# Layer 2's probabilities turned by a transposing DMA, and layer 1's value products and transposes put into one block

## The reference

```python
# layer 1, 12 heads of 64
h = einsum('bnd,ade->bane', x, W)
attn = leaky(tanh(h) @ w_src + swap(tanh(h) @ w_dst), 0.2)
attn = softmax(where(adj, attn, -999.0))
feat = elu(heads_joined(attn @ h + b))
gate = sigmoid(x @ H_w.T + H_b)
x = layernorm(x + gate * feat + (1 - gate) * x)
# layer 2, 6 heads of 128
q, k, v = heads(x @ Wq + bq), heads(x @ Wk + bk), heads(x @ Wv + bv)
probs = softmax(q @ k.T / sqrt(128) + where(adj, 0, -9e15))
x = layernorm(x + heads_joined(probs @ v) @ Wf + bf)
```

## Time and profile before

| | us |
|---|---|
| median of 3 runs | 2765.53 (2763.75 to 2770.96) |
| the profiled execution | 2766.33 |
| its span, first to last instruction | 2764.6 |
| PE busy | 2726.9 (99%) |
| DVE busy | 1668.8 (60%) |
| ACT busy | 1160.3 (42%) |
| POOL busy | 1066.3 (39%) |

### The profile page before, as it was taken

How to read it: one execution, slowest core, us unless ns; L and a number is a source line. 1 busy time by engine, 2 the same in 40 slices (tenths; PEclk the granted TensorE clock), 3 DMA queues, 4 the chain that set the end, 5 groups by cost and what they waited for, 6 DMA issues and landing times.

```text
span 2764.6 us, 51821 instructions
## 1 busy us (share of the span) xinstructions
PE 2726.9 (99%) x20988; PEld 2517.8 (91%) x20988; DVE 1668.8 (60%) x3334; ACT 1160.3 (42%) x3045; POOL 1066.3 (39%) x630
## 2 busy tenths in 40 slices
PE   8999999999999989999999999999999999999998
PEld 6877778888788889999999999999999999999998
DVE  6888998888888754444454444454445445444443
ACT  5666776666666633322332233322332233223322
POOL 2453344433444134433444343434443343434340
PEclk9999999999999999999999999999999999999999
DMA  5656665555555512222213222222222222222220
GB/s 180 173 131 145 164 160 145 139 139 139 141 137 143 175 59 69 69 71 81 70 58 81 76 75 58 79 72 71 69 68 71 81 70 58 81 81 70 58 70 23
DMA packets 306894, 269.49 MB, mean 97 GB/s; under 512 B 227808, under 2 KB 244192, under 8 KB 306656
## 3 DMA queue, kind: packets, MB, share of 16 engines
q1 hardware_dynamic: 306656, 266.19, 35.5%
HBM read 142.65 MB, written 75.89 MB: 79 GB/s over the span
## 4 chain that ended last, share of the span: by engine, by line
PE 85%; DVE 5%; DMA 4%; issue 2%; POOL 2%; ACT 2%; SPq 1%; DVEq 0%; ACTq 0%; POOLq 0%
PE ps_hg L1036 21%; PE ps_a L1199 14%; PE ps_k L70 14%; PE ps_q L70 14%; PE ps_a L70 14%; PE ps_c L1165 2%; PE ps_s L1140 2%; PE ps_pv L1068 1%; DMA dst_all<-dst_scratch 1%; ACT logits L564 1%; PE ps_t L1055 1%; PE ps_pt L1165 1%; DMA dst_scratch<-dst 1%; PE ps_pt L1147 1%; DVE logits L770 1%
## 5 line engine op out<-in xcount | busy, mean ns | idle before, releaser
L1036 PE MATMUL ps_hg<-w_hi,xT 128*128 128x512 f32 x2268 | 745.6, 401 | 8.3 <-DVE h_one L803 8.2
L1036 PEld LDWEIGHTS ps_hg<-w_hi,xT 128*128 128x128 f32 x2268 | 426.1, 188 | 112.6 <-issue 11.3
L1036 PE MATMUL ps_hg<-w_lo,xT 128*128 128x512 f32 x1134 | 448.4, 395 | 0.0
L70 PE MATMUL ps_k<-x1T_hi,wk_hi 128*128 128x256 f32 x1152 | 329.1, 286 | 0.0
L70 PE MATMUL ps_q<-x1T_hi,wq_hi 128*128 128x256 f32 x1152 | 323.5, 281 | 1.4 <-DVE x1T_lo L910 1.4
L70 PE MATMUL ps_q<-x1T_lo,wq_hi 128*128 128x256 f32 x1152 | 322.6, 280 | 0.0
L70 PE MATMUL ps_k<-x1T_lo,wk_hi 128*128 128x256 f32 x1152 | 321.9, 279 | 0.0
L70 PE MATMUL ps_q<-x1T_hi,wq_lo 128*128 128x256 f32 x1152 | 321.9, 279 | 0.0
L70 PE MATMUL ps_k<-x1T_hi,wk_lo 128*128 128x256 f32 x1152 | 321.1, 279 | 0.0
L496 POOL TENSOR_TENSOR th_src<-th,wsrc_all 128x768 f32<-128x768 f32 x64 | 118.3, 1848 | 483.7 <-DVE dst_all L783 463.4
L648 ACT ACTIVATE qT<-ps_q,bq_col 128x256 f32<-128x256 f32 x192 | 80.5, 470 | 479.3 <-PE ps_q L70 479.3
(11 more groups left out here) (144 smaller groups left out, 5814.2 us busy)
## 6 DMA issues: line engine op xcount, KB each, us to landing
x_tok<-x SPq DMA_DIRECT2D x64, 384.0 KB, 4.1
dst_all<-dst_scratch SPq DMA_DIRECT2D x128, 192.0 KB, 3.4
gate_scratch<-gate SPq DMA_DIRECT2D x64, 384.0 KB, 2.6
feat_scratch<-feat SPq DMA_DIRECT2D x128, 192.0 KB, 2.8
feat_in<-feat_scratch SPq DMA_DIRECT2D x62, 384.0 KB, 3.1
gate_in<-gate_scratch SPq DMA_DIRECT2D x62, 384.0 KB, 3.7
x_even<-x SPq DMA_DIRECT2D x16, 768.0 KB, 4.2
x_odd<-x SPq DMA_DIRECT2D x16, 768.0 KB, 4.4
```

The costliest lines, as they stand in the source:

```text
L70: ins = pe.matmul(out, left[a][c], right[b][c], start=(n == 0), stop=(n == len(terms) - 1))
L1036: ins = pe.matmul(ps_hg[:, cols], left[a][c], right[b][c], start=(c == 0 and n == 0), stop=(c == KC - 1 and n == 2))
```

## The change

It has two parts. In layer 2, from group 2 on, the probabilities of each pair are no longer transposed on TensorE: POOL splits `scores_sb` into two 16-bit planes (`split_p1`), SP turns them with a transposing DMA (`turn_p1`), and ACT and DVE join the planes into `probs1T` (`join_block`). POOL's list places the splits around the preparation of the next group's input, and DVE's mix of the second tile moves behind `logits_of(G, 2)` and `probs_out(G, 1)`. In layer 1, `values(T-2)` and `transpose_probs(T-1)` follow each other in the middle of `project(2)`; `copy_probs` moves behind the exponentials of the same tile on ACT, and `bias_h(T)` in front of `attention(T-2)` on DVE.

```diff
+        planes_p1 = at(S + 53184, "planes_p1", [P, 2, PN * NODES], U16)
+        planes_p1T = at(S + 54208, "planes_p1T", [P, 2, 2, P], U16)
...
+        def join_block(copy, buf, t, g, signal):
+            s = graph(g)
+            out_ = probs1T[s, buf, :, s].bitcast(U16).rearrange("p (h t) (n l) -> p l h t n", t=GT, l=2)[:, :, :, t, :]
+            copy(out_, planes_p1T[t * NODES:(t + 1) * NODES, :, :, s]).then_inc(signal, 1)
+        def pair_of(G, j):
+            return PAIRS * (G - BY_DMA) + j + 1
...
# SP
+            def turn_p1(G, j):
+                sp.wait_ge(split_p1_done, pair_of(G, j))
+                for joined_ in (ptc_act, ptc_dve):
+                    sp.wait_ge(joined_, 2 * (PAIRS * G + j))
+                sp.dma_start_transpose(planes_p1T.rearrange("p l h n -> p (l h) n"),
+                                       planes_p1.rearrange("p l (h m) -> p (l h) m", h=2)).then_inc(turned_p1, 16)
...
                     sp.dma_start(x1_tok[s][:, :, :], x_g[G + 2]).then_inc(x1_in[s], 16)
+                if BY_DMA <= G + 1 < NG:
+                    turn_p1(G + 1, 0)
+                if G + 2 < NG:
                     sp.wait_ge(mixed, GT * (G + 2) + 1)
                     feat_and_gate(G + 2, 1)
+                if BY_DMA <= G + 1 < NG:
+                    for j in range(1, PAIRS):
+                        turn_p1(G + 1, j)
...
# POOL
+            def split_p1(G, j):
+                pool.wait_ge(probs_done, PAIRS * G + j + 1)
+                if pair_of(G, j) > 1:
+                    pool.wait_ge(turned_p1, 16 * (pair_of(G, j) - 1))
+                pool.tensor_copy(planes_p1[:, :, :], scores_sb.rearrange("p k m -> p (k m)").bitcast(U16)
+                                 .rearrange("p (d l) -> p l d", l=2)).then_inc(split_p1_done, 1)
...
-                if 1 <= G < NG - 1:
-                    for t in range(GT):
+                for t in range(GT):
+                    if 1 <= G < NG - 1:
                         feat_less_x(G + 1, t, feat_in[:, :])
+                    if G >= BY_DMA:
+                        split_p1(G, t)
+                    if 1 <= G < NG - 1:
                         times_gate(G + 1, t, feat_in[:, :], gate_in[:, :])
+                if G >= BY_DMA:
+                    split_p1(G, GT)
...
# ACT, layer 1
-                if T >= 2:
-                    copy_probs(T - 2)
+                if T == 2:
+                    copy_probs(0)
...
                 exp_scores(T - 1)
                 if T >= 2:
+                    copy_probs(T - 1)
                     elu_exp(T - 2)
...
# ACT, layer 2
                 value_out(G, 0)
-                probs_out(G, 1)
+                if G < BY_DMA:
+                    probs_out(G, 1)
                 exps(G, 2)
+                if G >= BY_DMA:
+                    probs_out(G, 1)
...
# DVE, layer 1
                 dst_scores(T)
                 if T >= 2:
+                    bias_h(T)
                     attention(T - 2)
-                    bias_h(T)
...
# DVE, layer 2 (and logits_of(G, j) now waits for split_p1_done of pair j-1)
-                elif G + 1 < NG:
+                elif G < BY_DMA:
                     mix(G + 1, 1, feat_in[:, :])
                     input_moments(G + 1)
-                probs_out(G, 1)
+                if G < BY_DMA:
+                    probs_out(G, 1)
                 logits_of(G, 2)
+                if G >= BY_DMA:
+                    probs_out(G, 1)
+                    if G + 1 < NG:
+                        mix(G + 1, 1, feat_in[:, :])
+                        input_moments(G + 1)
...
# TensorE, layer 1
                 project(1, T).then_inc(h_done, 1)
+                project(2, T, range(KC // 2))
                 if T >= 2:
                     values(T - 2)
-                project(2, T).then_inc(g_done, 1)
-                if T >= 2:
                     transpose_probs(T - 1)
+                project(2, T, range(KC // 2, KC)).then_inc(g_done, 1)
...
# TensorE, layer 2: scores(G, j) waits for logit_done of pair j-1, and
-                transpose_probs1(G, 0)
+                if G < BY_DMA:
+                    transpose_probs1(G, 0)
```

More of the change, by code:

```diff
@@ L244, in two_graph_layers @@
         turned1 = [sem(f"turned1_{t}") for t in range(GT)]
+        split_p1_done, turned_p1 = (sem(n) for n in ("split_p1_done", "turned_p1"))
         v_done, v_copied, o_done, o_added = (sem(n) for n in ("v_done", "v_copied", "o_done", "o_added"))
@@ L677, in probs_out @@
             def probs_out(G, j):
-                act.wait_ge(pt1_done, PAIRS * G + j + 1)
-                for g in range(2):
-                    copy_block(act.copy, (G + j) % 2, 0, g, ptc_act)
+                if G < BY_DMA:
+                    act.wait_ge(pt1_done, PAIRS * G + j + 1)
+                    for g in range(2):
+                        copy_block(act.copy, (G + j) % 2, 0, g, ptc_act)
+                else:
+                    act.wait_ge(turned_p1, 16 * pair_of(G, j))
+                    for g in range(2):
+                        join_block(act.copy, (G + j) % 2, 0, g, ptc_act)
             def context_hi(G, j):
@@ L687, in _ @@
             round_x1(0)
-            copy_probs(NT - 2)
             leaky_scores(NT - 1)
@@ L916, in logits_of @@
                     dve.wait_ge(bias_mask, G + 1)
+                elif G < BY_DMA:
+                    dve.wait_ge(pt1_done, PAIRS * G + j)
                 else:
-                    dve.wait_ge(pt1_done, PAIRS * G + j)
+                    dve.wait_ge(split_p1_done, pair_of(G, j - 1))
                 dve.scalar_tensor_tensor(
@@ L934, in probs_out @@
             def probs_out(G, j):
-                dve.wait_ge(pt1_done, PAIRS * G + j + 1)
-                for g in range(2):
-                    copy_block(dve.tensor_copy, (G + j) % 2, 1, g, ptc_dve)
+                if G < BY_DMA:
+                    dve.wait_ge(pt1_done, PAIRS * G + j + 1)
+                    for g in range(2):
+                        copy_block(dve.tensor_copy, (G + j) % 2, 1, g, ptc_dve)
+                else:
+                    dve.wait_ge(turned_p1, 16 * pair_of(G, j))
+                    for g in range(2):
+                        join_block(dve.tensor_copy, (G + j) % 2, 1, g, ptc_dve)
             def context_lo(G, j):
@@ L1028, in transpose_x, with project @@
                 ins.then_inc(xT_done, 1)
-            def project(k, T):
+            def project(k, T, chunks=range(KC)):
                 cols = slice(k * BLK, (k + 1) * BLK)
@@ L1033, in project @@
                 right = [[t[:, c, cols] for c in range(KC)] for t in (w0_hi, w0_lo)]
-                for c in range(KC):
+                for c in chunks:
                     for n, (a, b) in enumerate(((0, 0), (0, 1), (1, 0))):
@@ L1132, in scores @@
             def scores(G, j):
+                if G >= BY_DMA:
+                    pe.wait_ge(logit_done, PAIRS * G + j)
                 pe.wait_ge(q_copied, 2 * (PAIRS * G + j + 1))
@@ L1243, in _ @@
                 value(G, 0)
-                transpose_probs1(G, 1)
+                if G < BY_DMA:
+                    transpose_probs1(G, 1)
                 scores(G, 2)
@@ L1248, in _ @@
                 first_context(G)
-                transpose_probs1(G, 2)
+                if G < BY_DMA:
+                    transpose_probs1(G, 2)
                 value(G, 3)
```

## The result

The changed kernel takes 2833.5 us (median of 4 runs, 2829.1 to 2841.1), against 2768.2 us for the kernel before, measured beside it. The ratio is 1.024, 95% interval 1.0221 to 1.026: slower by some 65 us, where the forecast was 9 us slower and its range ended at 2800. The profiled execution took 2841.06 us, at the upper end of the runs.

A forecast was written before the change was run, and what follows sets the result against it. TensorE, busy 99% of the span, was taken to bound the kernel. Removed transposes -19.8, layer 1 -3 and layer 2 stalls +31.9 gave +9.1 us on 2765.5, so 2774.6 us, range 2746 to 2800.

The forecast's parts named there:

- The removed transposes: Layer 2, TensorE: three pairs of transposes at 0.22 us each disappear in 30 groups, a gain of 19.8 us.
- The dates: Layer 2: step-by-step times of split, turn and join, ending with pair 2 joined at 2069.05, 0.85 us late.
- the join on DVE: Layer 2: DVE joins pair 2's planes after the turn lands at 2068.12, taking about 0.9 us.
- the lock-out: Layer 2: POOL's splits hold DVE's pair 2 join in half the groups, 12 to 23 us more; chance shared, 0.14.
- the slow transpose: Layer 2: transposing DMA lands after 4.0 us whatever its size, 32 us more, 2806 us; chance shared, 0.14.
- Who ends last: Layer 2: TensorE waits at pair 2's contexts for its joins, mean 1.1 us in 29 groups, 31.9 us lost.
- odd groups worse than even ones: Layer 2: pair 2's join is 1.34 us late in odd groups, against 0.85 us in the shown group.
- -3 us: Layer 1: fewer TensorE waits for `h_one`, 3 us gained, taken between 0 and 8.2 us.
- Side by side: Layer 1: placing transposes directly behind values could save or cost up to 11.8 us for switching; taken as 0.
- the 1.2 us to spare: Layer 1: transposes start at about 3.1 us, the exponentials they need are ready at 1.9 us.
- layer 1 turns: Layer 1: late exponentials stall every tile or the 0.19 us is paid twice, up to 12 us more; chance 0.06.
- The route is hidden: Layer 2: cheaper splits, turn and joins leave hardly any wait; all hidden gives 2742.7 us; chance 0.22.

The follow-up runs named there:

- layer 2's part alone: The changed kernel with its layer 1 edits undone, so layer 1 as before and layer 2 changed: 2825.7 us, ratio 1.0207.
- another order on DVE: Only layer 2's changes, with `normalise(G, 2)` ahead of the second mix, `context_lo(0)` and pair 2's join ahead of `input_norm`: 2750.6 us, ratio 0.9939.

## Why the prediction was wrong

*The removed transposes.* 19.8 us was right: with every wait at the contexts gone, layer 2's part gains 16 us, and the median group 0.63 of the 0.66 us.

*The dates.* Against the start of the group, forecast (for the group of rows 5 to 8) and trace (the group shown above): gate on POOL 17.0 and 16.9 us; split 1 28.6 and 28.4; second mix 33.5 and 33.6; split 2 38.1 and 38.3; ACT's join done 42.7 and 42.3. The split was put at 0.65 us (0.61), the turn at 2.9 (2.4), the join at 0.9 (0.98 on ACT, 0.66 on DVE if free). The agreement on the second mix is partly luck: POOL's gate ended some 0.4 us sooner than forecast, and the joins of pair 1, which the forecast left out of this path, put the mix 0.55 us behind it.

*The step that failed* is the join on DVE. The sum let it run freely once the turn had landed at 2068.12 of the shown group, beside POOL's splits, and kept the lock-out as a rival, for half of the groups and with 0.14 for it and the slow transpose together. It happens in all 29: TensorE waits 1.17 to 1.18 us for it in each, 34.0 us in sum, and in the group shown DVE's two joins take 2.16 us and not 0.66. The experiment that only moves POOL's split takes 47 us off. The same row that the prediction showed for the multiply, held until POOL ended, should have been charged to the join in the sum, since the forecast's own dates laid both on each other. The Trainium skill, "SBUF — State Buffer", section "SBUF: two separate sides", has the rule (a DVE operation in a two-port mode and a GpSimd operation lock each other out whole). The trace agrees, if the join runs in such a mode; no run here shows the mode.

*Who ends last.* The forecast had TensorE stop once a group, for pair 2's joins, 1.1 us in the mean and 31.9 us in sum. The 26.1 us of the other wait look like that figure, and that is luck: it is another wait. TensorE stops before pair 1's contexts, for `context_lo(0)`, which the prediction never dated. By its own dates there was no slack: with `normalise(G, 2)` done at 2064.45, the rest of the root (0.89 us in rows 6), `input_norm` (1.19) and `context_lo` (0.87, both from the trace) put its end at about 2067.4, an estimate, and with the 0.25 us that TensorE takes to go on this is 0.1 us behind 2067.53, when TensorE comes to pair 1's contexts. In the trace it is 0.6 us later still. Pair 2's joins are late too: in the group shown TensorE would have wanted them at about 2059.06, and ACT's were done at 2059.59, but the longer wait hides this one. Nor were odd groups worse than even ones, as forecast: this wait is 0.94 us in even groups and 0.86 in odd.

*What the stalls cost beyond themselves.* In layer 2's part alone the waits sum to 61.2 us; less 19.8 that is 41, and the loss was 59. I summed what the granted clock lacks to full in slices of 5 us between 1060 and 2740 us: 10 us in this kernel, nearly all in four dips that go down to 0.50, and none below 0.97 in the kernel before or in the one where POOL's split waits. The forecast had no term for it. The last 8 us or so, 0.3 us a group, stay open. No rival reached the result, the highest being 2806: the lock-out was charged to half of the groups, `context_lo` and the clock to none.

*Layer 1.* -3 us was forecast, +5 measured. "Side by side" was put at 0 and is worth 0.04 us a quiet tile, 2.5 us in all. The step that failed is the date of the transposes: the 1.2 us to spare was read in one tile, and it isn't there in the tiles with a late `dst`. The wait for `h_one` became one for the exponentials, and not a smaller one. Why the loop through the DMAs got longer is open: the load ahead of the store lengthens it, but did so before the change as well. The rival "layer 1 turns" had the sign and was given 0.06.

*The rivals.* "The route is hidden" can be had, but by another order on DVE, not by this change: 2750.6 us, against 2742.7 worked out with 3 us of layer 1 in it.

## What to carry to other kernels

Work moved off the bounding engine pays only if the last of it is ready in time. Write out the dates of the new path and of everything that stands behind it on the same engine (here `context_lo`), and then look at what runs on the neighbour at each step. Here a short DVE copy from SBUF beside a long POOL copy did not end before POOL's; put it ahead of the operation that releases POOL, as `input_norm` here. The gains don't add: the earlier normalise alone gave 11 us, POOL's later split alone 47, and the order that removes both waits 75. And check the name in a list of waits against the program: where an instruction waits for several semaphores, the list can name one that wasn't the last.

## What the runs showed of the hardware

A transposing DMA of four 128x128 blocks of 16 bits landed 2.4 us after its issue in the median (up to 4.0), one of twelve blocks 4.0 us. DVE joined 64 partitions x 256 16-bit elements from SBUF in 0.29 to 0.32 us, with reads in sequence or strided, and in both cases up to 1.74 to 1.77 us beside POOL. The block of values, which works in 64x64 tiles of the array, charges transposes behind it about as much as a product: a tile took 0.04 us less in sum, not the 0.19 that could have vanished. And two waits of TensorE within one slice of 5 us, 1.7 us in sum, were followed by 5 us at 0.66 of the full clock on average; this happened in some 4 of 29 groups with such waits.
